# Full-array products cut into four column tiles, expert biases as one bf16 product, and a new order of steps, in a two-layer attention and expert kernel on one core

## The chip, the cores and the metric

The kernel runs on 1 core of one Trainium2 chip. The metric is the time of one execution on the device in microseconds. TensorE is called PE here, VectorE DVE, ScalarE ACT, GpSimd POOL, and the queue that issues most transfers is SP.

## What is computed

Two layers run over 4 batches of 512 tokens of width 128, all in float32. Each layer adds an attention and a mixture of experts to its input; layer 0 has a whole block in place of the experts, with an attention of its own in front of them. That makes 12 attentions of 16 heads of width 8: types 0 and 1 (layer 0, causal) and type 2 (layer 1, not causal).

```python
xn = _layernorm(x)
x = x + attn0(xn) + block0(xn)     # block0: layernorm, attention, layernorm, 8 experts 128->512->128
xn = _layernorm(x)
x = x + attn1(xn) + moe1(xn)       # moe1: top 2 of 8 experts 128->128->128
# block0's experts (moe1 has the same form, its gates softmax values of all 8)
w   = softmax(where(logits >= second_largest, logits, -inf))
mid = gelu(h2 @ e_w1 + e_b1); eo = mid @ e_w2 + e_b2
moe = sum_e w[e] * eo[e]
```

The term that the change rewrites is the sum over experts of gate times output bias, `w @ e_b2`, a product with a contraction of 8.

## The kernel before

The work of the core is one list of steps, `order.plan`. Every engine walks the same list and takes its own part of each step, so the list sets the order on every engine and also that of the transfers on SP. The list is written out as a string, `SCORE`, of one letter for each step, with a digit where a step takes a bank of PSUM. The letters are: A the front of a batch (layer norms, turns, projections), M `max` (products whose row maximum DVE takes), T `max_turn` (the maxima turned and put back among the queries by a transfer), S `scores`, V `values`, H the division and the output projection of an attention, E and O `expert_in` and `expert_out` of layer 0, I and J the same of layer 1, F and G the norms and gates, K the transfers that fill a stack of query or key parts, L the transfers of expert weights. Seven banks of PSUM go round, an eighth holds the sums of `values`.

PE uses its array in three ways. `max` and `scores` are bf16 products with a contraction of 64 rows, two side by side (rows, below). `values` (L925) gives four heads at once a column tile of 32 columns each. All other products fill 128 rows and 128 columns (full): `expert_in` (L973), `expert_out` (L986), projections (L854, L857), `out_project` (L935), `route` (L945), `route_turn` (L953), `route_bias` (L960), turns (L841) and `max_turn` (L890). A float32 product appears in the trace as two instructions, each a weight load and a matmul, called passes here; so `expert_out` of layer 0, 8 products in a step, is 16 passes.

For an expert, PE's `expert_in` writes two banks, ACT applies Gelu into a slot of `probs`, PE's `expert_out` reads it, and DVE (L690) adds it, times the gate, to the accumulator. For `max`, PE writes two banks and DVE (L535) reduces them; for `scores`, ACT (L778) takes the exponential and, in causal attentions, POOL (L1071) clears half of the diagonal block. ACT's Exp and Gelu need different tables, and a change of table is a load (L730).

The expert bias: after DVE's `gate`, PE turns the gates with `ident` (`route_turn`), DVE copies them out (`gateT`, 8 x 512, L670), PE multiplies them with `ebias` (`route_bias`), and DVE adds the result (L677).

Of the kernel before, what the change touches and what calls it, by code (L numbers as in the profile page):

```python
# [11 lines left out]
P = 128  # L12
# [11 lines left out]
HALF = 64  # L24
PRODUCTS = ((0, 0), (0, 1), (1, 0), (0, 2), (1, 1), (2, 0))
MAX_BLOCK, ZERO_BLOCK, BLOCKS = 6, 7, 8
VALUE_ROWS, SUM_COL = 2 * HD, 1
# [70 lines left out]
AAAAAAAA6A6A0AAAKAKAKA1M2M4M0M2M4M0A6M2M4T6M0M2M4A6S0S2M4S0A6S2M4S0M2VKKAM0S4T6M2AVM0AVAM4M2A6S0M4LS2VM0T6S2AM4S0KM2  # L98
S4AM0VM2AM4S0S2M0AM4S2M0VM4S2S0T6S2VAVS4HM0M2VM4S0AT6S2ALVS4VS0VM2LM4AVS0S2VS4M0M2A6S4VVM0S2T4A6HS2M0VM4S2A6AM0S2S4V
S2VAM4S0M2KM4AS0KVT6M2M0S4VM2S4M0S4S2HKVLM4M0HS2VT6S4M2VM0M4S2VM0S2VM4S2M0S4HVHS2M0S4T6VM2M0S4VM2S4H6M0S4M2VS0M4HVVM  # L100
2HT6A0S4LM2A6S0S4HVS2HHM0A6S4S2A0AAAA1T6VS4M2S0VKHKVS4M2S0H6FS4M0FVS2S4VVVKS2M0S4VF6M2S4M0VE4F6AM2M0FM4VVE2FE0O6T0M4
M2HAM0OE4E2E0O6M4M2M0OE4O6T4AM2M0M4OE2E0E4T6E2E0O6S4AS2M0OF4E0O6S2AM4S0OE2M4M0O6S4M2AM0OO2E4E0OT6O3OF6S4S0VFM2AFS4S0
VVVM2S4S0HVF6M4S0S2VHVS0M4S2F6A0S4S2G1HF6S4FVGM2S0S4HVVHKVGVFM0S2I4I2H6FF4KT5A6S0S2S4FVHKA0AFI2I4F6M0M2VVVS4S0F6FJ2S
4S0J6M4AS2VVS0M2AM4G6E0A2A6M4KM0M2VVFA6E4A0KE2J1E4AT6F0J2O6M0M4S2OM0S2E4M2M0O6M2M4M0AOE2E4O6S0M2M4OE0S2M4F6T0J1E4KM2
M0O6AM2M4M0OE2HA0J6S4S2AM0VVM4S0M2O6S4M0M2VM4AS0OS2M0S4HVAHVS2M4E0T6E2E4AAE0E2E4M0M2O6T2M0M4M2OS0VM4S2HAS0O6M4M2S0VM
4M0S2VM4M2S0OS4S0M2VHS4M2S0H6S4M2VS0M4S2O6T2T3S0M4M2OM0S4S2FVVS4M0S2VS4S0KFVS2KM4VS0KS4M2VS0M2S4J6T0F1S2VM4S2S0F6HVS
4M2M0VVS4M2F6S0HS4M2VS0T6M4S2VS0HM4S2VM0VM2S4M0VS2HM4M0S2T6VM4FHM2S0J6S4M0S2VVM4S2VS0HKT6M2FFM4KKS0H6S2M0VM4S2G6S0M2
S4VM0GT6S2M4VM0I2AM4VM0S2HA6HVS4M0S2A6S4M0I2T6M4VVM0S2VM4S0G6S2M0S4HVVVS2S0M4A6S2GVHHS4M0S2VT6M4S0M2F6S4S0VVM2S4VHM0
S2S4GVVS2M0S4KJ6I2AI4M0M2VJ6H0S4S2J1T6S4FVS2M0S4VJ6S2M4HS0VVAS2M0KS4FJ6S2S0VVM4AS2F0A6S4M2HM0VVM4M2F6FKE0A2E4T6E2E0E
# [131 lines left out]
def build(nc, x, proj, w_expert_in, w_expert_out, w_in, w_out, routers, cols, row, expert_bias, out):  # L241
# [3 lines left out]
    with ctx:  # L245
# [97 lines left out]
        gpsimd_done = signal("gpsimd_done")  # L343
        cut = signal("cut")
        max_split = signal("max_split")
        keys_cleared = signal("keys_cleared")
        qk_sorted = signal("qk_sorted")
        v_cleared = signal("v_cleared")

# [866 lines left out]
```

## Time and profile before

| | |
|---|---|
| median of 3 runs | 742.12 us (741.61 to 742.81) |
| profiled execution, its own time | 742.59 us |
| its span in the profile | 740.0 us |
| PE busy, of the span | 711.5 us |
| DVE busy | 569.5 us |
| ACT busy | 509.3 us |
| POOL busy | 185.2 us |

The profile shows one execution. Ends of matmuls are modelled: each is shown longer than the pitch at which the next one starts, so PE's busy time hides waits of less than some 0.15 us, and what a pass costs is read from start to start. The time of a run is 2.6 us more than the span.

### The profile page before, as it was taken

The page shows a single profiled execution, that of the slowest core. Times are in us where ns is not written, and L with a number is a line of the kernel's source. Part 1 is how long each engine was busy: PE and PEld are TensorE (multiplying, and loading weights), DVE is VectorE, ACT ScalarE, POOL GpSimd, SP SyncE. Part 2 cuts the span into 40 slices and gives each one's busy share as a digit, 9 for nine tenths or more (in the row PEclk, how much of TensorE's full clock was granted, in tenths as well). Part 3 has the DMA queues.
Part 4 walks back from the last instruction along what each step waited for, and adds up shares of the span by engine and source line. Part 5 has one row for each costly group of instructions (what it writes and reads, how often), then busy time and mean ns, then how long its engine had stood idle before and what let it go on. Part 6 is the DMA issues. An engine that isn't in the chain of part 4 may idle for free.

```text
span 740.0 us, 15886 instructions
## 1 busy us (share of the span) xinstructions
PE 711.5 (96%) x6222; PEld 387.6 (52%) x6222; DVE 569.5 (77%) x1127; ACT 509.3 (69%) x632; POOL 185.2 (25%) x425
## 2 busy tenths in 40 slices
PE   5689999999999999999999999999999999999997
PEld 2333345667645665564544456567654666533345
DVE  5989998545788868688999967658778476788966
ACT  7266777366686567667789866764787748588882
POOL 5165546011343012103533200021372110010000
PEclk9699999999999999999999999999999999999999
DMA  6243523000132000004232200031031000030101
GB/s 155 53 140 129 164 93 110 11 19 1 34 96 79 3 25 17 19 5 111 64 88 69 62 3 19 4 99 31 5 93 54 9 11 17 3 94 13 28 25 39
DMA packets 42009, 38.75 MB, mean 52 GB/s; under 512 B 14312, under 2 KB 37232, under 8 KB 41712
## 3 DMA queue, kind: packets, MB, share of 16 engines
q1 hardware_dynamic: 40592, 36.17, 17.5%
q10 hardware_dynamic: 1152, 1.05, 0.6%
q8 instruction: 49, 0.80, 0.5%
q0 software_dynamic: 192, 0.52, 0.3%
q14 instruction: 24, 0.20, 0.1%
HBM read 10.47 MB, written 1.44 MB: 16 GB/s over the span
## 4 chain that ended last, share of the span: by engine, by line
PE 79%; DVE 9%; ACT 4%; DMA 4%; issue 2%; POOL 1%; SPq 1%; ACTq 1%; POOLq 0%; DVEq 0%
PE psum L986 19%; PE psum L973 18%; PE psum L925 15%; PE psum L904 8%; PE psum L877 8%; DVE neg_max L535 6%; PE psum L854 2%; PE psum L935 1%; PE psum L882 1%; DMA inverses<-heads_den 1%; PE psum L857 1%; PE psum L945 1%; PE psum L960 1%; ACT k_stack L716 1%; DVE acc L690 1%
## 5 line engine op out<-in xcount | busy, mean ns | idle before, releaser
L535 DVE TENSOR_REDUCE neg_max<-psum 128x2 f32<-128x1024 f32 (+2 forms) x320 | 344.9, 1113 | 82.2 <-PE psum L877 40.2
L778 ACT ACTIVATE probs<-psum 128x1024 f32<-128x1024 f32 (+1 forms) x320 | 287.1, 938 | 122.4 <-PE psum L904 120.7
L802 ACT ACTIVATE probs<-psum,col 128x512 f32<-128x512 f32 x160 | 100.5, 684 | 78.9 <-PE psum L973 78.3
L925 PE MATMUL psum<-probs,v_ones 128*32 128x512 f32 (+3 forms) x1536 | 152.8, 496 | 0.1
L986 PEld LDWEIGHTS psum<-ew,probs 128*128 128x128 f32 x1024 | 120.1, 192 | 17.6 <-issue 14.2
L986 PE MATMUL psum<-ew,probs 128*128 128x128 f32 x1024 | 129.1, 280 | 0.0
L877 PE MATMUL psum<-k_stack,q_stack 64*128 64x512 bf16 (+3 forms) x768 | 113.7, 333 | 13.6 <-DMA q_stack<-part 8.2
L1071 POOL TENSOR_SCALAR_AFFINE_SELECT probs<-probs 128x512 f32<-128x512 f32 x128 | 82.0, 646 | 176.7 <-ACT probs L778 176.6
L973 PE MATMUL psum<-normed_T_a,ew 128*128 128x512 f32 x256 | 118.0, 599 | 0.0
L904 PE MATMUL psum<-q_stack,k_stack 64*128 64x512 bf16 (+3 forms) x768 | 109.2, 330 | 3.9 <-DVE neg_max L535 1.2
L690 DVE SCALAR_TENSOR_TENSOR acc<-psum,gate,acc 128x128 f32<-128x128 f32 x256 | 71.9, 344 | 23.5 <-PE psum L986 21.7
L1057 POOL CAST max_part<-neg_max 128x16 bf16<-128x16 f32 x48 | 9.8, 205 | 298.2 <-DVE neg_max L535 282.8
L730 ACT ACT_TABLE_LOAD x63 | 80.8, 1283 | 1.1
L877 PEld LDWEIGHTS psum<-k_stack,q_stack 64*128 64x128 bf16 x768 | 36.5, 94 | 76.3 <-issue 24.8
L904 PEld LDWEIGHTS psum<-q_stack,k_stack 64*128 64x128 bf16 x768 | 31.7, 94 | 75.9 <-ACT probs L778 28.4
L973 PEld LDWEIGHTS psum<-normed_T_a,ew 128*128 128x128 f32 x256 | 45.6, 190 | 48.0 <-issue 42.9
L925 PEld LDWEIGHTS psum<-probs,v_ones 128*32 128x32 f32 x1536 | 35.8, 108 | 48.5 <-issue 33.2
L882 PEld LDWEIGHTS psum<-above,pick 64*128 64x128 bf16 x1024 | 44.9, 97 | 16.9 <-issue 1.4
L882 PE MATMUL psum<-above,pick 64*128 64x64 bf16 x1024 | 52.4, 193 | 0.0
L986 PEld LDWEIGHTS psum<-wout,probs 128*128 128x128 f32 x256 | 31.1, 191 | 8.2 <-issue 5.2
L986 PE MATMUL psum<-wout,probs 128*128 128x128 f32 x256 | 35.1, 282 | 0.0
L1040 POOL TENSOR_TENSOR part<-rest,part 128x512 bf16<-128x512 f32 x24 | 27.4, 1157 | 12.8 <-ACT part L759 11.6
(124 smaller groups left out, 494.2 us busy)
## 6 DMA issues: line engine op xcount, KB each, us to landing
q_stack<-part SPq DMA_DIRECT2D x66, 128.0 KB, 2.4
k_stack<-part SPq DMA_DIRECT2D x66, 128.0 KB, 2.4
heads_raw<-head_sums SPq DMA_DIRECT2D x24, 128.0 KB
heads_inv<-inverses SPq DMA_DIRECT2D x12, 256.0 KB, 3.3
ew<-w_expert_in SPq DMA_DIRECT2D x4, 512.0 KB, 4.9
ew<-w_expert_out SPq DMA_DIRECT2D x4, 512.0 KB, 6.7
q_stack<-k_stack SPq DMA_DIRECT2D x14, 128.0 KB, 2.3
q_stack<-maxT SPq DMA_DIRECT2D x48, 32.0 KB, 1.8
```

What stands on the lines that cost most here:

```text
L535: eng.tensor_reduce(neg_max[:, q % 2, :, xs[0]:xs[-1] + 1, i], src, AX_X, ALU.max, negate=True).then_inc(vector_done.sem, 1)
L690: eng.scalar_tensor_tensor(out=acc_of[b % 2][:, t, :], in0=src[:, t * P:(t + 1) * P], scalar=gate_of[layer][:, t, expert:expert + 1], in1= ...
L730: eng.preload_act_table(table)
L778: eng.activation(dst, src, ACT.Exp, scale=SCALE).then_inc(probs_ready.sem, 1)
L802: ins = eng.activation(probs[:, order.slot[step[:-1]], 2 * k + f, :], two_banks(step)[:, f, :], ACT.Gelu_apprx_tanh if layer else ACT.Gelu ...
L877: ins = eng.matmul(dst[:, a, col0:col0 + keys], q_stack[slot][rows_of, head, i * P:(i + 1) * P], k_stack[slot][rows_of, head, 0:keys], sta ...
L882: ins = eng.matmul(dst[:, a, col0:col0 + HALF], pick[rows_of, upper, :], above[rows_of, upper, :], start=False, stop=upper == 1)
L904: ins = eng.matmul(dst[:, a, n * width:(n + 1) * width], k_stack[slot][rows_of, head, j * P:(j + 1) * P], q_stack[slot][rows_of, head, TIL ...
L925: ins = eng.matmul(sum_bank[32 * c:32 * c + V_COLS, q0:TILES * P], v_ones[u][:, j, g // 2 * QH + c, col0:col0 + V_COLS], probs[:, order.sl ...
L973: ins = eng.matmul(dst[:, f, :], w, normed_T["y" if layer else "a"][:, :], start=True, stop=True)
L986: ins = eng.matmul(dst[:, t * P:(t + 1) * P], middle[:, f, t * P:(t + 1) * P], w, start=f == chunks[0], stop=f == chunks[-1])
L1071: eng.affine_select(out=diagonal, in_=diagonal, compare_op=ALU.is_ge, fill=no_chance, base=0, pattern=[[0, QH], [1, P]], channel_multiplie ...
```

## The change

Four things change. First, a helper `columns` issues each full product as four products of 32 columns of the kept operand, one for each column tile, with the same moving operand. It is used for projections, `out_project`, `route`, both expert steps and `max_turn`; the turns (L841) stay as they were. Second, the gates are split by POOL into three bf16 parts, six blocks of 8 (48 columns), and the biases once into a stack of 48 rows, which six small transfers on SP put together. `route_turn` becomes two bf16 products for each tile of tokens and `route_bias` one bf16 product with a contraction of 48 where it was a float32 product with 8. Third, `max_turn` writes float32 to PSUM where it wrote bf16. Fourth, the string `SCORE` is another one, with the same letters in the same numbers.

```diff
 SCORE = """
-AAAAAAAA6A6A0AAAKAKAKA1M2M4M0M2M4M0A6M2M4T6M0M2M4A6S0S2M4S0A6S2M4S0M2VKKAM0S4T6M2AVM0AVAM4M2A6S0M4LS2VM0T6S2AM4S0KM2
+AAAAAAAA6A6A0AAKAAAKA1KM2M4M0M2M4M0M2M4M0T6M2A4M0M2M4S0A6S2S0A4S2KM0T6M2AS4VAAM0M2VS4M0KAVM2M4M0S2A6M4S2M0AKM2VS4T6M
...
+            def columns(dst, kept, moving, start=True, stop=True):
+
+                for c in range(COLUMN_TILES):
+                    some = slice(COLUMN * c, COLUMN * c + COLUMN)
+                    ins = eng.matmul(dst[some, :], kept[:, some], moving, start=start, stop=stop)
+                return ins
...
-                    eng.transpose(dst, max_part[:, q % 2].rearrange("p a n c -> p (a n c)"),
-                                  ident16[:, :]).then_inc(work_full.sem, 1)
+                    ins = columns(dst, max_part[:, q % 2].rearrange("p a n c -> p (a n c)"), ident16[:, :])
+                    ins.then_inc(work_full.sem, 1)
...
                 elif kind == "route_turn":
-                    eng.wait_ge(vector_done.sem, order.dve["gate", b, step[2]])
+                    eng.wait_ge(gate_split.sem, 4 * (order.gates.index(step[1:]) + 1))
                     dst = bank(step)
+                    parts = gate_part_of[step[2]][:, :, :, :].rearrange("p t n e -> p t (n e)")
                     for t in range(TILES):
-                        ins = eng.transpose(dst[0:EXPERTS, t * P:(t + 1) * P], gate_of[step[2]][:, t, :], ident[:, :])
+                        for some in (slice(0, COLUMN), slice(COLUMN, GATE_ROWS)):
+                            ins = eng.matmul(dst[some, t * P:(t + 1) * P], parts[:, t, some], ident16[:, :],
+                                             start=True, stop=True)
...
                 elif kind == "route_bias":
                     eng.wait_ge(vector_done.sem, order.dve["route_turn", b, step[2]])
+                    if b == 0:
+                        eng.wait_ge(bias_landed.sem, 16 * len(BIAS_PARTS))
...
-                                         ebias[:, step[2], :], start=True, stop=True)
+                                         bias_stack[:, step[2], :], start=True, stop=True)
...
-                        ins = eng.matmul(dst[:, f, :], w, normed_T["y" if layer else "a"][:, :], start=True, stop=True)
+                        ins = columns(dst[:, f, :], w, normed_T["y" if layer else "a"][:, :])
...
-                            ins = eng.matmul(dst[:, t * P:(t + 1) * P], middle[:, f, t * P:(t + 1) * P], w,
-                                             start=f == chunks[0], stop=f == chunks[-1])
+                            ins = columns(dst[:, t * P:(t + 1) * P], middle[:, f, t * P:(t + 1) * P], w,
+                                          start=f == chunks[0], stop=f == chunks[-1])
...
+                elif kind == "route_turn":
+                    layer, n = step[2], order.gates.index(step[1:])
+                    gate, parts = gate_of[layer], gate_part_of[layer]
+                    eng.wait_ge(vector_done.sem, order.dve["gate", b, layer])
...
+                    eng.tensor_copy(parts[:, :, 0:3, :], gate[:, :, :].unsqueeze(2).to_broadcast([P, TILES, 3, EXPERTS]))\
...
+                    eng.tensor_tensor(gate_left[:, :, :], gate[:, :, :], parts[:, :, 0, :], ALU.subtract)\
...
+                    if piece == EXPERT_PIECES:
+                        eng.wait_ge(bias_split.sem, 4)
+                        for n, part_of in enumerate(BIAS_PARTS):
+                            eng.dma_start(bias_stack[EXPERTS * n:EXPERTS * (n + 1), :, :], bias_part[:, part_of])\
```

The order on PE, at the first experts of batch 0, before (L973 is `expert_in`, L986 `expert_out`, L925 `values`, L877 and L882 `max`; the count is of products):

```order
L925 MATMUL psum<-probs,v_ones 32x256 x4
L925 MATMUL psum<-probs,v_ones 32x128 x4
L973 MATMUL psum<-normed_T_a,ew 128x512 x4
L986 MATMUL psum<-ew,probs 128x128 x8
L890 MATMUL psum<-ident,max_part 128x128
L877 MATMUL psum<-k_stack,q_stack 128x384 x2
L882 MATMUL psum<-above,pick 128x64 x4
```

The same engine and place after the change (L845 is the helper `columns`, L896 and L901 `max`, L923 `scores`):

```order
L845 MATMUL psum<-ew,probs 32x128 x32
L845 MATMUL psum<-normed_T_a,ew 32x512 x8
L845 MATMUL psum<-ident,max_part 32x128 x4
L845 MATMUL psum<-normed_T_a,ew 32x512 x16
L845 MATMUL psum<-ew,probs 32x128 x32
L923 MATMUL psum<-q_stack,k_stack 128x512 x2
L896 MATMUL psum<-k_stack,q_stack 128x384 x2
L901 MATMUL psum<-above,pick 128x64 x4
```

The 8 products of an `expert_out` have become 32, and expert steps, `max_turn` and `values` now stand in one shape of the array, 32 columns wide, so that PE goes from one of them to the other without another shape between.

ACT at the same part of the program, before (L778 is the exponential of `scores`, L802 the Gelu of `expert_in`, L786 the copy of the sums, L759 the second part of a projection):

```order
L778 ACTIVATE probs<-psum 128x2x384
L730 ACT_TABLE_LOAD
L802 ACTIVATE probs<-psum,col 128x512 x4
L730 ACT_TABLE_LOAD
L778 ACTIVATE probs<-psum 128x2x384
L778 ACTIVATE probs<-psum 128x2x2x256
L778 ACTIVATE probs<-psum 128x2x2x128
L759 ACTIVATE part<-rest 128x512
L730 ACT_TABLE_LOAD
L802 ACTIVATE probs<-psum,col 128x512 x4
```

And after (L791, L815 and L799 are the same three, L743 the table load):

```order
L815 ACTIVATE probs<-psum,col 128x512 x8
L743 ACT_TABLE_LOAD
L791 ACTIVATE probs<-psum 128x1024
L743 ACT_TABLE_LOAD
L815 ACTIVATE probs<-psum,col 128x512 x2
L799 ACTIVATE head_sums<-psum 128x512
L743 ACT_TABLE_LOAD
L791 ACTIVATE probs<-psum 128x1024
L791 ACTIVATE probs<-psum 128x2x384
L743 ACT_TABLE_LOAD
```

The new order goes to and fro between exponential and Gelu more often: over the whole program ACT's list has 64 table loads before and 77 after.

POOL where batch 0's first gates are turned, after (L1083 and L1085 end the split of the maxima, L1114 to L1123 split the gates, L1098 begins the split of the biases):

```order
L1083 CAST max_part<-max_rest 128x2x8
L1085 TENSOR_TENSOR max_part<-max_rest,max_part 128x2x8
L1114 CAST gate_part<-gate 128x4x24
L1117 TENSOR_TENSOR gate_left<-gate,gate_part 128x32
L1120 CAST gate_part<-gate_left 128x4x16
L1123 TENSOR_TENSOR gate_part<-gate_left,gate_part 128x4x8
L1098 CAST bias_part<-ebias 8x256
```

Before, nothing of the gates and biases was on POOL; now eight groups of four, and one of four for the biases, stand among its other steps.

## Rows read from the trace of the kernel before

**Rows 1.** The page's head and busy times of each engine.

```profile
span 740.0 us, 15886 instructions
PE 711.5 (96%) x6222; PEld 387.6 (52%) x6222; DVE 569.5 (77%) x1127; ACT 509.3 (69%) x632; POOL 185.2 (25%) x425
```

**Rows 2.** Busy time by stretch, with clock and DMA.

```profile
0.00:20.00 20.00, 9.64 (x30) 4.00 (x30) 10.90 (x47) 14.59 (x30) 11.11 (x35) 0.93 0.62 157
20.00:100.00 80.00, 69.13 (x911) 30.68 (x911) 75.48 (x113) 47.56 (x62) 38.40 (x86) 0.91 0.39 115
100.00:720.00 620.00, 617.40 (x5185) 342.75 (x5182) 469.53 (x925) 440.97 (x534) 135.74 (x305) 1.00 0.15 42
720.00:740.00 20.00, 15.38 (x106) 10.21 (x104) 13.64 (x45) 6.23 (x8) 0.00 (x0) 0.93 0.11 36
```

**Rows 3.** What PE waited for: total us, times, longest.

```profile
PE psum L877 <- DMA q_stack<-part: 8.2, 1, 8.2
PE psum L877 <- DVE neg_max L535: 2.8, 7, 0.8
PE psum L890 <- POOL max_part L1063: 1.6, 2, 1.4
```

**Rows 4.** Timeline of PE, full-array runs, each with what follows.

```profile
177.10 3.84 PE L986 MATMUL psum<-ew,probs 128*128 128x128 f32 x32
180.77 1.02 PE L973 MATMUL psum<-normed_T_a,ew 128*128 128x512 f32 x2
...
249.75 1.98 PE L973 MATMUL psum<-normed_T_a,ew 128*128 128x512 f32 x4
251.67 0.60 PE L877 MATMUL psum<-k_stack,q_stack 64*128 64x512 bf16 x4
...
718.36 2.05 PE L986 MATMUL psum<-wout,probs 128*128 128x128 f32 x16
720.34 0.39 PE L904 MATMUL psum<-q_stack,k_stack 64*128 64x512 bf16 x2
```

**Rows 5.** Timeline of PE, column-tile runs, each with what follows.

```profile
203.89 0.43 PE L925 MATMUL psum<-probs,v_ones 128*32 128x128 f32 x8
204.25 0.39 PE L877 MATMUL psum<-k_stack,q_stack 64*128 64x512 bf16 x2
...
707.40 1.06 PE L925 MATMUL psum<-probs,v_ones 128*32 128x512 f32 x8
708.40 0.61 PE L904 MATMUL psum<-q_stack,k_stack 64*128 64x512 bf16 x4
...
711.78 1.92 PE L925 MATMUL psum<-probs,v_ones 128*32 128x512 f32 x16
713.64 0.39 PE L904 MATMUL psum<-q_stack,k_stack 64*128 64x512 bf16 x2
```

**Rows 6.** Timeline of the weight loads of the run at 707.40.

```profile
707.40 0.16 PEld L925 LDWEIGHTS psum<-probs,v_ones 128*32 128x32 f32 x8 [0.23 <-issue]
```

**Rows 7.** Groups of PE by line and shape, route and bias products.

```profile
L960 PE MATMUL psum<-ebias,gateT 8*128 8x128 f32 x64 | 9.2, 283 | 0.0
L945 PE MATMUL psum<-router,normed_T_y 128*128 128x8 f32 x32 | 4.2, 259 | 0.0
```

**Rows 8.** ACT's table loads, and PE's instruction queue, from the page.

```profile
L730 ACT ACT_TABLE_LOAD x63 | 80.8, 1283 | 1.1
q8 instruction: 49, 0.80, 0.5%
```

**Rows 9.** Timeline of POOL, first and last of one split.

```profile
27.55 0.19 POOL L1057 CAST max_part<-neg_max 128x16 bf16<-128x16 f32 x1 [8.76 <-DVE neg_max L535]
...
28.38 0.22 POOL L1063 TENSOR_TENSOR max_part<-max_rest,max_part 128x16 bf16<-128x16 f32 x1
```

**Rows 10.** The chain that ended last, its final PE and DVE pieces.

```profile
728.40 0.91 PE psum L986 x8
...
736.55 0.69 DVE acc L567
```

More of the change, by code:

```diff
@@ L186, in __init__ @@
         self.projects = [step[1:] for step in plan if step[0] == "parts"]
+        self.gates = [step[1:] for step in plan if step[0] == "route_turn"]
         self.layers = [step[1:] for step in plan if step[0] == "gate"]
@@ L308, in build @@
         gate_of = [sb(f"gate{n}", [P, TILES, EXPERTS]) for n in range(2)]
[L309 removed]
+        gate_part_of = [sb(f"gate_part{n}", [P, TILES, len(BIAS_PARTS), EXPERTS], BF16) for n in range(2)]
+        gate_left = sb("gate_left", [P, TILES, EXPERTS])
+        gateT_of = [sb(f"gateT{n}", [GATE_ROWS, TILES * P], BF16) for n in range(2)]
+        bias_part = sb("bias_part", [EXPERTS, PARTS, 2, P], BF16)
+        bias_left = sb("bias_left", [EXPERTS, 2, P])
+        bias_stack = sb("bias_stack", [GATE_ROWS, 2, P], BF16)
         psum = ctx.enter_context(nc.psum_tensor("psum", [P, 8, 512], F32))
@@ L853, in _ @@
                     if k < 2:
-                        ins = eng.matmul(dst, proj_qk[:, u, k, :], src[:, :], start=True, stop=True)
+                        ins = columns(dst, proj_qk[:, u, k, :], src[:, :])
                     else:
                         for t in range(TILES):
-                            ins = eng.matmul(dst[:, t * P:(t + 1) * P], src[:, t * P:(t + 1) * P],
-                                             projs[:, u, 0, :], start=True, stop=True)
+                            ins = columns(dst[:, t * P:(t + 1) * P], src[:, t * P:(t + 1) * P], projs[:, u, 0, :])
                     ins.then_inc(work_full.sem, 1)
@@ L934, in _ @@
                     for t in range(TILES):
-                        ins = eng.matmul(dst[:, t * P:(t + 1) * P], headsT[:, t * P:(t + 1) * P],
-                                         projs[:, step[2], 1, :], start=True, stop=True)
+                        ins = columns(dst[:, t * P:(t + 1) * P], headsT[:, t * P:(t + 1) * P], projs[:, step[2], 1, :])
                     ins.then_inc(work_full.sem, 1)
@@ L944, in _ @@
                     for t in range(TILES):
-                        ins = eng.matmul(dst[:, t * EXPERTS:(t + 1) * EXPERTS], src[:, t * P:(t + 1) * P],
-                                         router[:, layer, :], start=True, stop=True)
+                        ins = columns(dst[:, t * EXPERTS:(t + 1) * EXPERTS], src[:, t * P:(t + 1) * P], router[:, layer, :])
                     ins.then_inc(work_full.sem, 1)
```

78 lines of the change are left out of this document (55 added, 23 removed).

## The prediction

> **What bounds the kernel now.** I read the page's head first: PE is busy for 711.5 of 740.0 us, DVE for 569.5 and ACT for 509.3 [rows 1]. Then the stretches: from 100 to 720 us PE is busy 617.40 of 620 at the full clock, while DVE has 469.53 and ACT 440.97 [rows 2]. So the bulk is bound by PE's own work and the other two have room on the average. Before 100 us it is otherwise: from 20 to 100 us DVE is busy 75.48 of 80 and PE 69.13, at a mean clock of 0.91 [rows 2]. PE's waits tell the same. The one long one, 8.2 us, is the first fill of the stacks; waits on DVE come to 2.8 in seven pieces [rows 3]. The tail is DVE's: PE's last run on the chain begins at 728.40, and the chain ends with the addition at 736.55 [rows 10]. A microsecond taken from PE between 100 and 720 us should shorten the run, one taken in the opening or behind the last product mostly not.
>
> **What a pass and a visit cost now.** By start to start, 32 passes of 128 moving columns take 3.67 us and 16 take 1.98 with the way in and out [rows 4]. The first gives (3.67 - 0.10)/32 = 0.112 a pass if entering costs 0.10; then 1.98 - 16 x 0.112 = 0.19 for entering and leaving. For 512 columns, 4 passes take 1.92; with 0.43 a pass that leaves 0.20 [rows 4]. I use 0.112, 0.43 and 0.20 a visit.
>
> The column-tile runs of the values are the model for the new products, since they also put four tiles of 32 columns through one pass. There, 8 instructions of 512 columns (two passes of four tiles) take 1.00 and 16 take 1.86, so a pass of four tiles is 0.43, as much as one full pass, and a visit 0.14 [rows 5]. At 128 columns, 8 instructions take 0.36: less 0.14 that is 0.11 a pass [rows 5]. So a product in column tiles costs the same or a trace less, and a visit is 0.06 cheaper. The reason that the rows give: the weights of a tile are a quarter as wide, and the eight loads of the run at 707.40 are over 0.16 us after its start, the second four under the first pass [rows 6].
>
> **The change part by part.** Counts are from the list of steps in both orders.
>
> Visits: PE enters the full shape 146 times before, 23 after (the turns and the bias products stay full); it enters the column shape 136 times before, 244 after. That is 146 x 0.20 + 136 x 0.14 = 48.2 us against 23 x 0.20 + 244 x 0.14 = 38.8: -9.4 us. Leaving the row pairs (max, scores) is paid whichever shape follows, 258 against 252 times: nothing.
>
> Passes of 128 columns: 1472 (expert_out 1280, value and output projections 96 each). By the row they cost 0.11 +- 0.005 where they cost 0.112: I take 0.0025 less, -3.7 us, with bounds -10 and +4. Passes of 512 (expert_in 320, projections 48): 0.43 in both, 0. The 64 passes of route move only 8 columns, and each loads 128 columns of weights: 32 are 4.2 us busy, 0.13 a pass [rows 7]. Narrow loads in four tiles should cut that; between 0 (as a pass of 128) and -5 (0.03 a pass) I take -2, since eight narrow loads are over in 0.16 us, 0.08 for four [rows 6], and 64 x (0.11 - 0.08) is 2.
>
> Biases: 64 passes at 0.112 (9.2 us busy in all [rows 7]) become 32 in bf16 of 128 columns, for which half a float32 pass, 0.056, is the estimate: -5.4 us. The gate turns, 32 passes of some 0.11, become 32 bf16 pairs of tiles of half that: -1.7. max_turn, one bf16 product in both, only changes shape; its visit is counted above.
>
> PE's work thus changes by -9.4 - 3.7 - 2 - 5.4 - 1.7 = -22.2 us.
>
> POOL: eight gate splits. A split of the maxima takes 28.60 - 27.55 = 1.05 us [rows 9]; the gates' parts are twice to six times as many elements in small pieces, so 1.1 to 3 us each, 9 to 24 us on an engine that is busy 185.2. The shortest way from a gate to its turn in the new order still has some 7 us of PE work in it, so nothing waits for it. If that cover were gone it would be 2 us in eight places. Behind the split on POOL stand the clearings of the diagonal and max splits, for which values and max_turn wait; they would be held only where DVE's gate is late. The bias split and six transfers stand once on SP ahead of a head sort: 0 to 3 us once, in a stretch where PE has work; I take 0. DVE copies 48 rows by 512 where it copied 8 by 512, and lanes work side by side: 0.
>
> ACT: 13 more table loads of 1.283 us are 16.7 us [rows 8]. They lie beside PE's work: ACT between 100 and 720 us would be busy 458 of some 600, 76%. If they all came to stand on the path, they would take back 16.7.
>
> Instructions: PE's grow from 12,444 weight loads and matmuls to 24,156. The queue that brings them moved 0.80 MB in 49 packets, 0.5% of the engines [rows 8]; twice that is still little. Nothing.
>
> What is given back: about 2 us of the saved PE work lies in the first 60 us of its work, where DVE sets the pace, and 1 us behind the last values, where DVE does. Then the waits. Only 2.6 us of PE idle time show between 100 and 720 us [rows 2]; DVE's same 469.5 us would stand against some 600, 78% where it is 76%, and the new order has maxima closer together around the first experts of batch 1. I add 4 us of new waits (no row has them: from 0, if the order spreads them well, to 12, most of what table loads add to ACT). Sum: -22.2 + 2 + 1 + 4 = -15.2. The profiled execution took 742.59, 2.6 more than its span, and stands 0.5 over the median; a difference of the span carries over as it is. 742.1 - 15.2 = 726.9, given as **727 us**.
>
> **A rule against it.** The rows show a column run whose second four loads are done under the first pass over the same 128 rows, and no load is exposed from pass to pass: 16 instructions less 8 are 0.86 for two passes, 0.43 each [rows 5, 6]. The Trainium skill, TensorE: Matmul & The Clock Gate, Part 3, The mechanism, has it that a weight load overlaps a running matmul only where the row group differs, and all four column tiles share their rows. By that rule each pass would expose a load, and the kernel would end as in the third rival below; the trace of `values` speaks against it.
>
> **The rivals.** *Forecast*, the PE work saved mostly shows: 716 to 734, chance 0.68. For it: the 620 us in which PE hardly waits.
>
> *Given back by DVE or ACT.* The new order packs maxima and table loads so that banks come free late. For it: DVE is at 75.48 of 80 in the opening, and 16.7 us of loads are added; against it: the averages of 78 and 76%. With 12 us of waits in place of 4 and 4 of ACT's 16.7 on the path: 727 + 12 = 739, chance 0.12, between 734 and 740.5.
>
> *Slower: column passes in long runs don't keep up.* The values never show more than four steps in a row, and an expert_out would be 128 instructions in 16 x 0.11 = 1.76 us, 0.014 each. A full visit is 0.06 dearer than a column one for three times 32 more columns to load, so an exposed load of 32 columns is some 0.02; exposed in each of 1,840 passes (1472 + 368) it would add 37 us: 764. It decides from 15/1840 = 0.008 us a pass. Against it: the eight loads within 0.16 us [rows 6], and 0.43 a pass over four passes [rows 5]. Chance 0.08.
>
> *No change*, the two sides cancel within 1.5 us: 742, chance 0.03.
>
> *More than forecast*: route passes at 0.03 and 128-column passes at 0.107 give 3 + 3.7 more (1472 x 0.0025), and waits no larger than today 4: 727 - 10.7 = 716, chance 0.09, from there down.
>
> **How the numbers follow.** What a measurement of this kernel tells from no change is about 0.2%, 1.5 us. Faster by more than that: 0.68 + 0.12 + 0.09, less 0.02 for the edge = 0.87. Same: 0.03 + 0.02 = 0.05. Slower: 0.08. The range for 8 in 10 reaches down to 716, where the larger gain begins, and up to 738, into the second rival (about half of its 0.12): 0.68 + 0.06, and half of the larger gain, which lies close under 716 if its terms come only in part, make 0.79. What is outside is the slow case, no change, and the ends.
>
> **What would show it.** Start to start, expert_out's step (16 passes of four tiles) and one visit should take 16 x 0.11 + 0.14 = 1.90 us between row products where they took 1.98, and expert_in's 4 passes 1.86 where they took 1.92. The four route_bias products should take some 0.22 us where they took 0.90. PE's idle time between 100 us and the end should stay below 8 us; ACT should show 76 table loads beside the first one, 97.5 us. The prediction is wrong if a 16-pass run takes 2.1 us or more (third rival), or if PE's waits on DVE's maxima or ACT's exponentials in the bulk reach 12 us (second).

## The result and the profile after

The changed kernel takes **723.52 us**, the median of 4 runs (722.89 to 724.07); the kernel before takes 742.46 over its 4 (741.61 to 743.08). The ratio is 0.9744, with a 95% interval of 0.9729 to 0.9759: 2.6% faster. The forecast was 727, the range 716 to 738.

The page's head of the kernel after, which answers to [rows 1]: span, then busy time of each engine.

```profile
span 721.1 us, 27651 instructions
PE 686.5 (95%) x12078; PEld 344.1 (48%) x12078; DVE 571.8 (79%) x1127; ACT 527.9 (73%) x645; POOL 194.1 (27%) x461
...
q8 instruction: 95, 1.56, 0.9%
...
L743 ACT ACT_TABLE_LOAD x76 | 97.5, 1283 | 1.3
```

PE has 25 us less to do, DVE 2 more, ACT 19 more, POOL 9 more, and the span is 18.9 shorter. So what the other engines got was almost all beside PE's work. The instructions nearly doubled, and the queue that brings them moved 95 packets instead of 49 [rows 8]; ACT has the 76 table loads beside the first.

The same by stretch, which answers to [rows 2]: PE, PEld, DVE, ACT and POOL busy, then the granted clock, the DMA share and GB/s.

```profile
0.00:20.00 20.00, 9.28 (x66) 3.63 (x66) 10.89 (x47) 14.48 (x30) 11.15 (x35) 0.91 0.62 157
20.00:100.00 80.00, 69.22 (x994) 30.78 (x996) 76.44 (x112) 47.46 (x61) 38.19 (x84) 0.89 0.31 88
100.00:702.00 602.00, 594.52 (x10714) 301.21 (x10714) 473.41 (x937) 459.86 (x547) 144.79 (x343) 1.00 0.17 48
702.00:721.10 19.10, 13.48 (x316) 8.48 (x312) 11.10 (x33) 6.09 (x8) 0.00 (x0) 0.96 0.13 39
```

The first 100 us are as they were. The whole gain lies behind them: PE was busy 617.40 of 620 us in the bulk and is now busy 594.52 of 602, so its idle time there went from 2.6 to 7.5 us.

What PE waited for, in total, times and longest, which answers to [rows 3]:

```profile
PE psum L896 <- DMA q_stack<-part: 9.3, 2, 8.3
PE psum L845 <- DVE headsT L570: 3.3, 2, 2.0
PE psum L896 <- DVE neg_max L548: 3.1, 8, 0.5
PE psum L896 <- ACT probs L791: 2.6, 7, 0.7
PE psum L923 <- DVE neg_max L548: 2.4, 6, 0.6
```

The waits are still small pieces. The largest new one is that for `headsT`, before the last output projection; the timeline of PE in the tail shows it, start and length, with the idle time before it in brackets:

```profile
716.52 1.08 PE L845 MATMUL psum<-projs,headsT 128*32 128x128 f32 x32 [1.97 <-DVE headsT L570]
```

**Two sums for reading the runs.** PE's busy time hides short waits and counts the modelled ends of its instructions. I therefore priced every PE product by start-to-start times of undisturbed runs in the traces of before and after: a pass of 128 columns 0.112 us in full shape and 0.109 in columns, one of 512 columns 0.429 in both, a bf16 pass of 128 columns 0.056, and going from the row pairs to columns and back 0.02 and 0.12, to full shape and back 0.10 and 0.09. The sum over PE's list is called *work* below; as a sum of many small prices it is an estimate, good to some 1 us. What is left of the time from PE's first product to its last is called *waits*; it holds the first fill of the stacks and the slower clock of the opening, too. Before: work 681.9, waits 45.9. After: work 656.5, waits 53.0. Ahead of PE's first product lie 7.9 us before and 7.8 after, and behind the start of its last one 4.3 before and 3.8 after. So the difference of the spans, -18.9, is -25.4 of work, +7.1 of waits and -0.6 at the two ends.

### The profile page after: what moved, and what is told of

The parts are those of the page before. It is cut to its first block, busy times and chain, and to the rows that moved or that the text cites. A ratio compares the mean times of both kernels' runs of the same rounds, so it can differ in the third digit from the quotient of the medians.

```text
span 721.1 us, 27651 instructions
## 1 busy us (share of the span) xinstructions
PE 686.5 (95%) x12078; PEld 344.1 (48%) x12078; DVE 571.8 (79%) x1127; ACT 527.9 (73%) x645; POOL 194.1 (27%) x461
## 3 DMA queue, kind: packets, MB, share of 16 engines
q10 hardware_dynamic: 1152, 1.05, 0.6%
## 4 chain that ended last, share of the span: by engine, by line
PE 78%; DVE 10%; ACT 5%; DMA 2%; issue 2%; SPq 2%; POOL 1%; ACTq 0%; POOLq 0%; DVEq 0%
PE psum L845 44%; PE psum L944 15%; PE psum L923 9%; PE psum L896 8%; DVE neg_max L548 6%; ACT probs L791 2%; SPq L395 2%; PE psum L901 1%; ACT k_stack L729 1%; DMA q_stack<-part 1%; PE psum L861 1%; ACT probs L815 1%; DVE acc L703 1%; DMA heads_inv<-inverses 1%; DMA q_stack<-maxT 1%
## 5 line engine op out<-in xcount | busy, mean ns | idle before, releaser
L548 DVE TENSOR_REDUCE neg_max<-psum 128x2 f32<-128x1024 f32 (+2 forms) x320 | 344.5, 1111 | 57.4 <-PE psum L901 31.1
L791 ACT ACTIVATE probs<-psum 128x1024 f32<-128x1024 f32 (+1 forms) x320 | 288.2, 939 | 108.2 <-PE psum L923 106.2
L944 PE MATMUL psum<-probs,v_ones 128*32 128x512 f32 (+3 forms) x1536 | 158.0, 494 | 0.0
L815 ACT ACTIVATE probs<-psum,col 128x512 f32<-128x512 f32 x160 | 100.8, 686 | 57.7 <-PE psum L845 57.3
L896 PE MATMUL psum<-k_stack,q_stack 64*128 64x512 bf16 (+3 forms) x768 | 114.9, 333 | 17.1 <-DMA q_stack<-part 9.3
L845 PE MATMUL psum<-ew,probs 128*32 128x128 f32 x4096 | 124.4, 274 | 0.0
L845 PEld LDWEIGHTS psum<-ew,probs 128*32 128x32 f32 x4096 | 109.7, 110 | 18.8 <-issue 17.1
L845 PE MATMUL psum<-normed_T_a,ew 128*32 128x512 f32 x1024 | 117.1, 593 | 0.8 <-DVE neg_max L548 0.7
L923 PE MATMUL psum<-q_stack,k_stack 64*128 64x512 bf16 (+3 forms) x768 | 110.7, 329 | 5.2 <-DVE neg_max L548 2.4
L743 ACT ACT_TABLE_LOAD x76 | 97.5, 1283 | 1.3
L896 PEld LDWEIGHTS psum<-k_stack,q_stack 64*128 64x128 bf16 x768 | 36.9, 95 | 83.8 <-issue 27.8
L923 PEld LDWEIGHTS psum<-q_stack,k_stack 64*128 64x128 bf16 x768 | 32.0, 94 | 80.7 <-issue 26.2
L845 PEld LDWEIGHTS psum<-normed_T_a,ew 128*32 128x32 f32 x1024 | 33.3, 110 | 58.2 <-issue 50.3
L901 PEld LDWEIGHTS psum<-above,pick 64*128 64x128 bf16 x1024 | 45.9, 97 | 16.4 <-issue 1.4
L901 PE MATMUL psum<-above,pick 64*128 64x64 bf16 x1024 | 52.9, 194 | 0.0
L845 PE MATMUL psum<-wout,probs 128*32 128x128 f32 x1024 | 33.7, 275 | 0.1
L845 PEld LDWEIGHTS psum<-wout,probs 128*32 128x32 f32 x1024 | 26.7, 110 | 8.4 <-issue 5.2
```

The costliest lines, as they stand in the source:

```text
L548: eng.tensor_reduce(neg_max[:, q % 2, :, xs[0]:xs[-1] + 1, i], src, AX_X, ALU.max, negate=True).then_inc(vector_done.sem, 1)
L743: eng.preload_act_table(table)
L791: eng.activation(dst, src, ACT.Exp, scale=SCALE).then_inc(probs_ready.sem, 1)
L815: ins = eng.activation(probs[:, order.slot[step[:-1]], 2 * k + f, :], two_banks(step)[:, f, :], ACT.Gelu_apprx_tanh if layer else ACT.Gelu ...
L845: ins = eng.matmul(dst[some, :], kept[:, some], moving, start=start, stop=stop)
L896: ins = eng.matmul(dst[:, a, col0:col0 + keys], q_stack[slot][rows_of, head, i * P:(i + 1) * P], k_stack[slot][rows_of, head, 0:keys], sta ...
```

## The experiments

Each run has its own runs of the kernel before on the same chip, from which the ratio is; their medians are 742.46, 741.90, 741.98 and 742.04 us, so kernels of different chips can be compared to some 0.6 us. The intervals are 1 to 3 us wide to either side, and differences of 2 or 3 us between two kernels are near what the runs can tell. The work and waits are the two sums above. Where the shapes of a kernel made them hard to price, they are left out.

| kernel | order | median us | ratio (95%) | span | work | waits |
|---|---|---|---|---|---|---|
| before | old | 742.46 | 1 | 740.0 | 681.9 | 45.9 |
| columns alone | old | 733.70 | 0.9888 (0.9866 to 0.9910) | 731.7 | 668.6 | 50.9 |
| biases alone | old | 759.62 | 1.0239 (1.0210 to 1.0269) | 758.9 | 676.3 | 70.5 |
| order alone | new | 753.36 | 1.0148 (1.0120 to 1.0177) | 753.4 | 694.1 | 47.5 |
| columns and biases | old | 748.89 | 1.0103 (1.0060 to 1.0146) | 746.5 | 658.6 | 75.8 |
| the same, gates split earlier | old | 734.89 | 0.9899 (0.9873 to 0.9924) | 731.8 | 658.6 | 61.0 |
| columns and order | new | 732.26 | 0.9864 (0.9836 to 0.9892) | 728.7 | 666.5 | 50.6 |
| after | new | 723.52 | 0.9744 (0.9729 to 0.9759) | 721.1 | 656.5 | 53.0 |
| after, gates split earlier | new | 724.64 | 0.9756 (0.9732 to 0.9779) | 722.9 | 656.5 | 54.8 |
| after, `max_turn` full | new | 727.29 | 0.9805 (0.9775 to 0.9834) | 725.3 | 663.0 | 50.7 |
| after, `route` full | new | 726.02 | 0.9797 (0.9757 to 0.9837) | 724.5 | 663.2 | 49.7 |
| after, no Gelu tables | new | 721.61 | 0.9726 (0.9690 to 0.9763) | 718.2 | 656.5 | 50.1 |
| after, `route_bias` in columns | new | 726.87 | 0.9790 (0.9762 to 0.9817) | 724.6 | | |
| after, tiles of 64 columns | new | 734.82 | 0.9900 (0.9866 to 0.9933) | 735.8 | | |

### The three parts, each by itself

Column tiles alone: the kernel after, with the string of before and the bias products of before.

```diff
 SCORE = """
-AAAAAAAA6A6A0AAKAAAKA1KM2M4M0M2M4M0M2M4M0T6M2A4M0M2M4S0A6S2S0A4S2KM0T6M2AS4VAAM0M2VS4M0KAVM2M4M0S2A6M4S2M0AKM2VS4T6M
+AAAAAAAA6A6A0AAAKAKAKA1M2M4M0M2M4M0A6M2M4T6M0M2M4A6S0S2M4S0A6S2M4S0M2VKKAM0S4T6M2AVM0AVAM4M2A6S0M4LS2VM0T6S2AM4S0KM2
...
-                    eng.wait_ge(gate_split.sem, 4 * (order.gates.index(step[1:]) + 1))
+                    eng.wait_ge(vector_done.sem, order.dve["gate", b, step[2]])
...
-                                         bias_stack[:, step[2], :], start=True, stop=True)
+                                         ebias[:, step[2], :], start=True, stop=True)
```

> The order and the biases of before, with every full product but the turns, the gate turns and the bias products in four column tiles. Theory (PE's own work, priced by visits and passes): counting this order with 0.19 to 0.20 a full visit, 0.14 a column visit, 0.109 and 0.112 a pass and 0.03 a route pass gives 14.3 us less PE work; with some 3 us of new waits, 731 us. Rival (the new order is what brings the gain, column tiles alone leave the waits where they were): 740 us or more.

Measured 733.70, 8.2 less than before on the same chip (741.90) and 2.7 over the expected 731; work is 13.3 less and waits 5.0 more, where 3 were expected. So column tiles bring a gain of their own, without the new order.

Biases alone: the string and the full products of before.

```diff
-                        ins = columns(dst[:, f, :], w, normed_T["y" if layer else "a"][:, :])
+                        ins = full(dst[:, f, :], w, normed_T["y" if layer else "a"][:, :])
```

> The order and the full products of before, with the biases in bf16 with 48 rows and POOL's splits. Theory (PE's own work): 5.2 us less, so 737 to 738 us. Rival (the detour over POOL holds up the turns or POOL's other steps): 742 us or more, with PE waiting for the gate split.

Measured 759.62, 17.7 *more* than before on the same chip (741.90), though PE's work fell by 5.6. The expectation of my own theory missed by over 20 us, and the rival, the way through POOL, was right. What PE waited for in this kernel:

```profile
PE psum L976 <- POOL gate_part L1127: 9.8, 3, 4.4
```

Three of the eight gate turns (L976) wait for the split, 9.8 us together. POOL's own timeline at the first of them shows why:

```profile
169.21 0.64 POOL L1097 TENSOR_SCALAR_AFFINE_SELECT probs<-probs 128x512 f32<-128x512 f32 x1 [11.47 <-ACT probs L791]
169.79 0.27 POOL L1118 CAST gate_part<-gate 128x96 bf16<-128x96 f32 x1
...
170.77 0.24 POOL L1127 TENSOR_TENSOR gate_part<-gate_left,gate_part 128x32 bf16<-128x32 f32 x1
```

The split itself takes 1.2 us, and it starts without a wait of its own. But ahead of it in POOL's list stands the clearing of a diagonal, and POOL had sat 11.47 us there until ACT's exponential came. PE's turn started at 171.07, 1.96 us after PE could have. Behind these waits PE ran at a lower granted clock for a time; by stretch (columns as above), in the same kernel:

```profile
100.00:200.00 100.00, 94.47 (x838) 60.84 (x840) 58.73 (x140) 57.00 (x73) 27.41 (x62) 0.98 0.14 40
200.00:300.00 100.00, 93.29 (x683) 53.21 (x675) 78.65 (x167) 63.72 (x82) 27.71 (x57) 0.98 0.17 46
300.00:400.00 100.00, 98.20 (x1024) 48.88 (x1024) 83.43 (x146) 73.67 (x87) 26.81 (x63) 1.00 0.19 53
```

The three hundreds with a wait for the split (100 to 300 and 500 to 600) have 0.98 of 2.4 GHz, the one from 300 to 400 has 1.00, as the whole bulk before [rows 2]. In finer stretches the clock is 0.50 (1.2 GHz) for some 3.4 us from 171.4, 243.1 and 509.4, right behind the three waits, of 1.96, 4.42 and 3.38 us. At half the clock PE does up to 1.7 us less in each, so they cost up to 5 us on top of the waits.

Order alone: before, with the new string.

```diff
-AAAAAAAA6A6A0AAAKAKAKA1M2M4M0M2M4M0A6M2M4T6M0M2M4A6S0S2M4S0A6S2M4S0M2VKKAM0S4T6M2AVM0AVAM4M2A6S0M4LS2VM0T6S2AM4S0KM2
+AAAAAAAA6A6A0AAKAAAKA1KM2M4M0M2M4M0M2M4M0T6M2A4M0M2M4S0A6S2S0A4S2KM0T6M2AS4VAAM0M2VS4M0KAVM2M4M0S2A6M4S2M0AKM2VS4T6M
```

> The kernel before with only the string of steps exchanged for the new one. Theory (the new order is made for column tiles): with full products it has 57 changes from values to full and 54 back where the old order had 16 and 8, which is 13.3 us more PE work: 754 to 758 us. Rival (the order is the better one by itself): 742 us or less.

Measured 753.36, 11.5 more than before on the same chip, just under the expected range and far from the rival. Work is 12.2 more and waits 1.6: the new order puts expert steps beside `values` and `max_turn`, which saves a change of shape only if both have the column shape. With full products it costs one.

### The order against the other two parts

The kernel after with the old string (the reverse of the line above, in the kernel after).

> The kernel after the change with the old string of steps. Theory (PE's own work): 2.3 us more than the kernel after the change, 725 to 728 us. Rival (the new order's spacing is worth much): 733 us or more, PE waiting for DVE and ACT in the bulk.

Measured 748.89, over 20 us more than expected, in the rival's range; what PE waited for most is POOL, which neither had named. Its work is 658.6, 2.1 over that of after, and its waits are 75.8, 22.8 over. The first row of PE's waits:

```profile
PE psum L972 <- POOL gate_part L1123: 10.0, 3, 4.4
```

Here the clock was at 1.2 GHz for 3.4 us from 115.2, behind a wait of 2.6 us for `headsT`, and for 6.8 and 3.4 us behind the waits of 4.42 and 3.45 for the split; behind the third, of 2.12, it stayed at 2.4 GHz.

The other side of the square: after, with the bias products of before (the second piece of the first diff).

> The kernel after the change with the biases done as before (float32 turns of the gates, float32 products with 8 rows, no splits on POOL). Theory (PE's own work; in the new order the splits are hidden): 9.2 us more PE work, of it 7 in the products themselves and the rest in changes of shape, so 731 to 734 us. Rival (the bias change costs about what it saves in any order): 724 us or less.

Measured 732.26: in the new order the bias part is worth 8.7 us (732.26 against 723.52) and its work is 10.0 less; in the old order with columns the same part costs 15.2 (733.70 against 748.89). Read the other way, with columns and the old bias products the new order is worth only 1.4 us (733.70 against 732.26), which the intervals do not tell from nothing.

Now the place of the split alone. POOL makes it at the step `gate`, where DVE makes the gates, instead of at `route_turn`; otherwise this is the kernel of the old order with columns and biases.

```diff
-        self.gates = [step[1:] for step in plan if step[0] == "route_turn"]
+        self.gates = [step[1:] for step in plan if step[0] == "gate"]
...
-                elif kind == "route_turn":
+                elif kind == "gate":
                     layer, n = step[2], order.gates.index(step[1:])
```

> The kernel after the change with the old string of steps, as in e4_old_order, but POOL splits the gates at its gate step, not at the route_turn step. Theory (PE waits at route_turn because POOL reaches the split only behind diagonal clears that wait for ACT): the three waits for the split, 10 us, and the fall of the clock behind them go: 728 to 736 us. Rival (the bf16 detour itself is slow, or something else holds the old order up): 744 us or more.

Measured 734.89, 14.0 less than with the split at `route_turn`, with the same work. The longest of PE's waits now, behind the first fill of the stacks:

```profile
PE psum L845 <- DVE headsT L570: 4.7, 2, 2.8
```

The row of `gate_part` is gone, and the clock is 1.00 in every hundred from 100 to 700 us. What stays is the wait for `headsT`, whose longest is 2.8 where it was 0.8 with the old biases in the same order. SP's list shows the reason, with the time that SP spent in issuing:

```profile
104.58 4.09 SPq L1174 DMA_DIRECT2D bias_stack<-bias_part  x6
108.72 0.45 SPq L1205 DMA_DIRECT2D inverses<-heads_den  x1
110.30 0.59 SPq L1209 DMA_DIRECT2D heads_inv<-inverses  x1
```

The six small transfers of the biases hold SP for 4.09 us, directly ahead of the transfer of the inverses, for which the division and then the output projection at 112 us wait. With the old biases that transfer is issued at 106.10 and the division starts at 112.63; here it starts at 113.95, and PE comes 0.7 us earlier. That makes the 2.0. In the kernel after, the same six take 4.13 us at 172.09, and SP's next issue is at 179.97: nobody is behind them.

Moving the split does not make the bias part pay in the old order: 734.89 stands against 733.70 with the old biases, though work is 10.0 less. PE's idle time is 9.8 us more (38.0 against 28.2): 3.3 in waits for `headsT`, 2.1 for ACT's exponentials, 2.3 for two norms, 1.2 for a transfer of maxima, the rest smaller.

The same edit in the kernel after:

> The kernel after the change, new order, but POOL splits the gates at its gate step. Theory (in the new order the split at the route_turn step is covered already, and POOL at gate waits longer for DVE with clears behind it): 723 to 726 us, no gain. Rival (the place at route_turn still costs hidden waits): 721 us or less.

Measured 724.64, no gain: in the new order PE's waits have no row of `gate_part`, and its place is worth nothing that the runs can tell.

### Single terms of the sum

`max_turn` full and in bf16 again, in the kernel after.

```diff
-                    ins = columns(dst, max_part[:, q % 2].rearrange("p a n c -> p (a n c)"), ident16[:, :])
-                    ins.then_inc(work_full.sem, 1)
+                    eng.transpose(dst, max_part[:, q % 2].rearrange("p a n c -> p (a n c)"),
+                                  ident16[:, :]).then_inc(work_full.sem, 1)
```

> The kernel after the change with max_turn left as one full-array bf16 transpose. Theory (changes of shape are what PE pays for): the 48 turns then stand as visits of another shape between column runs, 11 us more PE work though no product gets longer: 733 to 736 us. Rival (the gain is in the passes themselves): 724 us, no change.

Measured 727.29, 3.8 over the kernel after, and below what was expected. The direction holds and the size does not: 48 visits of 0.20 us alone would be 9.6. By start to start, a bf16 product adds no time on entering the full shape, only some 0.10 on leaving; the 0.10 for entering belongs to float32. With 48 x 0.10 and 13 more runs of columns to enter and leave at 0.14 that is 6.6, the 6.5 of the table; 2.3 of it comes back as shorter waits.

`route` full again, in the kernel after.

```diff
-                        ins = columns(dst[:, t * EXPERTS:(t + 1) * EXPERTS], src[:, t * P:(t + 1) * P], router[:, layer, :])
+                        ins = eng.matmul(dst[:, t * EXPERTS:(t + 1) * EXPERTS], src[:, t * P:(t + 1) * P],
+                                         router[:, layer, :], start=True, stop=True)
```

> The kernel after the change with route's products left full. Theory (a route pass costs 0.031 us in column tiles and 0.112 full, and a full visit among column runs costs two changes): 5 us from 64 passes and 1.7 us from changes: 728 to 731 us. Rival (route stands where PE has slack): 724 us.

Measured 726.02, 2.5 over the kernel after by the medians and 3.9 by the ratios. Its work is 6.7 more, and its waits are 3.3 less: PE's time saved at the router partly comes back as waiting.

`route_bias` in column tiles too.

```diff
-                        ins = eng.matmul(dst[:, t * P:(t + 1) * P], gateT_of[step[2]][:, t * P:(t + 1) * P],
-                                         bias_stack[:, step[2], :], start=True, stop=True)
+                        ins = columns(dst[:, t * P:(t + 1) * P], gateT_of[step[2]][:, t * P:(t + 1) * P],
+                                      bias_stack[:, step[2], :])
```

> The kernel after the change with route_bias in column tiles too, so that eight full-array visits go. Theory (changes of shape): 1.1 us less PE work, 721.5 to 723.5 us, hardly to be told from the kernel after the change. Rival (bf16 in column tiles loads its weights more slowly and loses that again): 724 us.

Measured 726.87, slower than the kernel after by 3.4 instead of faster. The timelines of PE at the first of them, kernel after:

```profile
182.62 0.34 PE L923 MATMUL psum<-q_stack,k_stack 64*128 64x384 bf16 x2
182.80 0.27 PE L982 MATMUL psum<-bias_stack,gateT 48*128 48x128 bf16 x2
182.86 0.28 PE L896 MATMUL psum<-k_stack,q_stack 64*128 64x256 bf16 x1
182.91 0.27 PE L982 MATMUL psum<-bias_stack,gateT 48*128 48x128 bf16 x2
...
183.45 0.75 PE L845 MATMUL psum<-ew,probs 128*32 128x128 f32 x20
```

and with `route_bias` in columns:

```profile
182.91 0.34 PE L923 MATMUL psum<-q_stack,k_stack 64*128 64x384 bf16 x2
183.18 0.41 PE L845 MATMUL psum<-bias_stack,gateT 48*32 48x128 bf16 x16
183.52 0.28 PE L896 MATMUL psum<-k_stack,q_stack 64*128 64x256 bf16 x2
...
183.96 1.74 PE L845 MATMUL psum<-ew,probs 128*32 128x128 f32 x56
```

From the scores to the next expert product lie the same products; they take 183.45 - 182.62 = 0.83 us in the one and 183.96 - 182.91 = 1.05 in the other. In the kernel after, a `max` product starts while two bias products are still to start: with 48 rows the bias product counts as one of the row pairs' shape, enters it at no cost and has a neighbour beside it. In columns it does not join the other column tiles either. `values` just ahead of it, in the kernel with `route_bias` in columns:

```profile
707.17 1.10 PE L944 MATMUL psum<-probs,v_ones 128*32 128x512 f32 x8
708.19 0.40 PE L845 MATMUL psum<-bias_stack,gateT 48*32 48x128 bf16 x16
```

Two passes of 0.43 take 1.02 us before the bias products of 48*32, as much as before row products (1.00, [rows 5]): from 128*32 to 48*32 is a change of shape too. So no visit goes, against what I had expected; one kind of visit replaces another. Over the eight places, from the last product ahead to the first behind, columns cost 0.22, 0.22, 0.22, 0.11, 0.11, 0.11, 0.14 and 0.01 us more: 1.1 in all. The profiled execution also waits 2.39 us at 644 for a transfer of key parts, for which that of the kernel after did not wait. The kernel after with the split at `gate` waits 1.66 there, with the same products as the kernel after; so this wait need not belong to the edit, and 2.3 of the 3.4 us is within the two intervals.

No Gelu tables: ACT applies Exp in place of both forms of Gelu, so that no table is changed in the bulk.

> The kernel after the change with Exp in place of both Gelus, so that ACT never changes its table: this leaves the Gelu out, and takes 76 table loads, 97.5 us, from ACT. Theory (ACT lies beside PE and the waits for it are small): 719 to 723 us. Rival (the table loads of the new order cost what DVE and ACT give back): 715 us or less.

Measured 721.61, its span 2.9 shorter. ACT's busy time falls from 527.9 to 431.7 us, and the kernel gains 2 us or so by the medians, inside the intervals of the two. So 97.5 us of table loads, 16.7 of them new, are hidden but for some 2 us, which the intervals do not tell from nothing.

Tiles of 64 columns, two in place of four.

```diff
-COLUMN = 32
+COLUMN = 64
```

> The kernel after the change with two column tiles of 64 in helper columns in place of four of 32; the values keep their tiles of 32. Theory (every change of tile shape costs PE some 0.1 us to leave, and the new order has about 110 changes between values and the other products): some 10 to 15 us more PE work though passes cost the same: 734 to 742 us. Rival (only the full 128-column shape is a shape of its own, or only the load of the first weights matters): 724 to 728 us.

Measured 734.82, 11.3 over the kernel after (its profiled execution, at 737.50, is the slowest of its four). Its runs between row products, by PE's timeline:

```profile
420.61 1.94 PE L845 MATMUL psum<-normed_T_a,ew 128*64 128x512 f32 x8
422.48 0.61 PE L896 MATMUL psum<-k_stack,q_stack 64*128 64x512 bf16 x4
423.01 1.97 PE L845 MATMUL psum<-ew,probs 128*64 128x128 f32 x32
424.91 0.61 PE L896 MATMUL psum<-k_stack,q_stack 64*128 64x512 bf16 x4
```

1.87 and 1.90 us, no more than 0.02 over the runs of 32 columns (below). The passes and the visits cost the same; what is lost is that `values` keeps its tiles of 32, so that another step beside it is again a change of shape. The same `max_turn` between two `values`, in the kernel after and then with tiles of 64:

```profile
691.87 1.07 PE L944 MATMUL psum<-probs,v_ones 128*32 128x512 f32 x8
692.75 0.24 PE L845 MATMUL psum<-ident,max_part 128*32 128x128 bf16 x4
692.81 1.04 PE L944 MATMUL psum<-probs,v_ones 128*32 128x512 f32 x8
```

```profile
705.25 1.07 PE L944 MATMUL psum<-probs,v_ones 128*32 128x512 f32 x8
706.24 0.25 PE L845 MATMUL psum<-ident,max_part 128*64 128x128 bf16 x2
706.42 1.06 PE L944 MATMUL psum<-probs,v_ones 128*32 128x512 f32 x8
```

The first `values` take 0.88 us and then 0.99, the turn 0.06 and then 0.18. PE's timeline has 54 such changes from 32 to 64 and 54 back; float32 passes of 512 columns ahead of one start 0.522 us before the next product where they are 0.429, in both directions. 108 x 0.093 is 10.0 of the 11.3.

## Why the prediction was right, and where it was off

**What bounds.** Right: PE's work in the bulk. Work fell by 25.4 us, and 18.9 of it came through.

**A visit and a pass in columns.** Right. The timeline of PE in the kernel after, one `expert_out` with row products around it and one `expert_in` the same:

```profile
160.68 1.96 PE L845 MATMUL psum<-ew,probs 128*32 128x128 f32 x64
162.56 0.28 PE L923 MATMUL psum<-q_stack,k_stack 64*128 64x128 bf16 x4
...
412.44 1.92 PE L845 MATMUL psum<-normed_T_a,ew 128*32 128x512 f32 x16 [0.43 <-DVE neg_max L548]
414.29 0.61 PE L896 MATMUL psum<-k_stack,q_stack 64*128 64x512 bf16 x4
```

1.88 us where 1.90 was forecast and 1.98 was before [rows 4], and 1.85 where 1.86 was forecast and 1.92 was before. With 0.109 a pass the 1472 passes of 128 columns give -4.4, where the sum has -3.7.

**The third rival, column passes that don't keep up in long runs**, is refuted by a long run without a change of shape:

```profile
301.93 1.96 PE L845 MATMUL psum<-ew,probs 128*32 128x128 f32 x64
303.70 1.90 PE L845 MATMUL psum<-normed_T_a,ew 128*32 128x512 f32 x16
305.42 0.84 PE L845 MATMUL psum<-projs,headsT 128*32 128x128 f32 x24
```

The 64 instruction pairs of the first row are 16 passes in 1.77 us, and then come 4 passes of 512 columns in 1.72: 0.111 and 0.43 a pass, 0.028 us for a pair of load and matmul, with no load exposed. The rule of the Trainium skill (TensorE: Matmul & The Clock Gate, Part 3, The mechanism), that a weight load overlaps a running matmul only where the row group differs, does not describe these runs: all four tiles share their rows. The same section of the Trainium skill also lets a load go ahead that targets the background weight buffer; whether these do, no row here can show.

**Route.** This term was mis-sized: -2 in the sum, -5.2 measured. The timeline of before, and then that of after, each with what follows:

```profile
201.73 1.06 PE L945 MATMUL psum<-router,normed_T_y 128*128 128x8 f32 x8
202.64 1.10 PE L854 MATMUL psum<-normed_T_y,proj_qk 128*128 128x512 f32 x2
```

```profile
411.01 0.46 PE L845 MATMUL psum<-router,normed_T_a 128*32 128x8 f32 x32
411.40 0.39 PE L896 MATMUL psum<-k_stack,q_stack 64*128 64x512 bf16 x2
```

Eight passes took 0.91 us, no more than 0.11 each though they move only 8 columns. In four tiles they take 0.39, of which 0.12 is leaving the shape: 0.03 a pass, the lower of the two bounds. I had taken the time of eight narrow loads from [rows 6] as their pitch; they go faster than that row shows.

**Biases.** The passes themselves came as forecast (a bf16 pass of 128 columns is 0.056). The step *the turns and the bias products stay full* was wrong: the product with 48 rows runs in the shape of the row pairs, and eight visits more are saved, 1.6 us by the forecast's price. Before, it had 8 rows, not 128, and cost what a full product costs: its 8 passes take 1.09 us with the way in and out, as 8 x 0.112 + 0.19 do. The four products take 0.22 us as forecast. The whole bias part saves 10.0 of work (666.5 to 656.5 in the table), against 5.4 + 1.7 in the sum.

**Visits.** -9.4 forecast. What is left of -25.4 after passes (-4.4), route (-5.2), biases (-5.4) and gate turns (-1.8) is -8.6, the extra bias visits included. So errors of both signs stand in it: a full visit in bf16, as `max_turn` made 48 of, cost some 0.1 less than the 0.20 used for it.

**What is given back.** The sum had 2 in the opening, 4 of new waits and 1 at the end: 7. Measured: waits up to 100 us of PE's time +0.9, behind that +6.2, the two ends -0.6: 6.5. The total is right, the place is not, and that two errors cancel in it is luck: the opening cost half of what I allowed and the bulk more. PE's idle time from 100 us to the end, 7.5 + 5.6 = 13.1 us by the stretches, is over the 8 that I named as the mark; before it was 2.6 + 4.6 [rows 2]. In the whole run it grew by 6.7 us (24.4 to 31.1), of which 2.1 are waits for maxima, 2.0 for `headsT` and 1.1 for the first fill. Neither of the second rival's causes reached its mark of 12: in the whole run, waits on maxima are 6.1 us (3.1 + 2.4 in the rows above, and smaller ones), and those on exponentials 2.6.

**The splits on POOL: right for this order, with the wrong reason.** I wrote that the shortest way from a gate to its turn still has some 7 us of PE work, so nothing waits. That says when DVE is ready. It says nothing about when POOL comes to the split, and in the old order POOL stands at a clearing that waits for ACT: 9.8 and 10.0 us of waits in three places, a lower clock after most of them, and 14.0 us gained by moving the split alone. I had looked at what the split might hold up behind it, not at what holds it up in front; that PE never waits for the split in the order of this change was luck as far as the forecast goes. In the new order what stands ahead on POOL at the first gates is a split of maxima that was released 0.77 us after POOL came to it, and POOL ended the gates' split at 167.25, 1.7 us before PE's turn at 168.94:

```profile
165.02 0.20 POOL L1079 CAST max_part<-neg_max 128x16 bf16<-128x16 f32 x1 [0.77 <-DVE neg_max L548]
...
167.00 0.25 POOL L1123 TENSOR_TENSOR gate_part<-gate_left,gate_part 128x32 bf16<-128x32 f32 x1
```

**The bias transfers.** *0 to 3 us once, I take 0*: SP is held for 4.1, over the upper end. It costs nothing in the new order, and in the old a wait of 0.8 became one of 2.8 behind it.

**The parts do not add up.** Alone they give -8.2, +17.7 and +11.5, together +21; the measured change is -18.9. With columns and biases in, the new order is worth 25.4 us (748.89 against 723.52). Of that, 14.0 could be had in the old order by moving the split, with what the clock lost after the waits in it; some 2 are fewer changes of shape; the rest, some 9, is in waits, of which the rows show 6.9 us (38.0 against 31.1 of PE's idle time) in many small pieces. Since the order is worth only 1.4 without the bias part, nearly all of the 25.4 hangs on the two together: the new order gives the bias part room, and what in that order does so, beyond the wait for the split, is not shown.

So the sum -22.2 + 7 stood at -15.2 and the span moved by -18.9: 3.2 of the 3.7 between them are PE's work, the route term above all, and 0.5 is what is given back.

## What to carry to other kernels

Price an array shape by visits and by the pass, from start to start, and per data type: here small moving operands (8 columns) and short runs gained most from column tiles, and long passes gained nothing. An order and a tiling are one decision, and each may look bad alone: this order was 1.5% slower with full products and this bias product 2.4% slower with the old order, for the most part by where one helper step stood. Before a step is put on an in-order engine that has slack, read what stands ahead of it in that engine's list and what that waits for; the distance between the producer and the consumer says nothing about it.

## What the hardware did that I had not expected

- A float32 pass of 8 moving columns takes 0.11 us with a full weight load and 0.03 with four loads of 32 columns. The moving columns are the same, so what differs is how the weights go in.
- A bf16 product of the full shape costs nothing on entering and 0.10 us on leaving; float32 costs 0.10 and 0.09.
- Going from 32-column tiles to 64-column tiles or back costs 0.093 us (0.522 for a last pass of 0.429), like any other change of shape, and so does going from 128*32 to 48*32.
- A product with 48 rows runs beside a row-pair product: a `max` product started at 182.86 between bias products of 182.80 and 182.91.
- Between 100 and 700 us, the four PE waits of 3.4 to 4.4 us were each followed by 3.4 or 6.8 us at 1.2 GHz. Of six waits of 2.0 to 2.8 us two were (1.96 at 171.07 in biases alone, 2.64 at 114.63 in columns and biases) and four were not (2.57 and 2.12 in the same kernels, 2.77 with the split moved, 2.39 with `route_bias` in columns). The waits of the kernel after, up to 1.3 us there, left the clock at 1.00.
- With nearly twice as many PE instructions (12,444 to 24,156), idle time of PE that no row puts down to a releaser came to 0.8 us in two pieces; before there was none over 0.15 us.
